# Attention in a fused two-layer kernel: the probability-times-value products issued in pairs in every second step

## The reference, cut to what matters

```python
q = jnp.einsum('bsd,hdk->bhsk', embeddings, Wq) + bq[None, :, None, :]
k = jnp.einsum('bsd,hdk->bhsk', embeddings, Wk) + bk[None, :, None, :]
v = jnp.einsum('bsd,hdk->bhsk', embeddings, Wv) + bv[None, :, None, :]
scores = jnp.einsum('bhqk,bhsk->bhqs', q, k) / jnp.sqrt(jnp.float32(dk))
scores = jnp.where(causal_mask, jnp.float32(-1000000000.0), scores)
weights = jax.nn.softmax(scores, axis=-1)
ctx = jnp.einsum('bhqs,bhsk->bhqk', weights, v)
```

## Time and profile before

| | us |
|---|---|
| median of 3 runs (1653.32 to 1657.09) | 1654.23 |
| the profiled execution, its own time | 1653.79 |
| its span in the trace | 1652.0 |
| attention stage, first to last product | 958.4 to 1438.2 |
| busy in the whole span: PE, PEld | 1332.8, 717.1 |
| busy in the whole span: DVE, ACT, POOL | 1195.5, 920.5, 932.1 |
| products (L2405), 1536 matmuls, busy | 163.7 |
| row maxima (L2103), 624 reductions, busy | 370.1 |

### The profile page before, as it was taken

How to read it: one execution, slowest core, us unless ns; L and a number is a source line. 1 busy time by engine, 2 the same in 40 slices (tenths; PEclk the granted TensorE clock), 3 DMA queues, 4 the chain that set the end, 5 groups by cost and what they waited for, 6 DMA issues and landing times. The chain is left out here.

```text
span 1652.0 us, 25211 instructions
## 1 busy us (share of the span) xinstructions
PE 1332.8 (81%) x7251; PEld 717.1 (43%) x7251; DVE 1195.5 (72%) x2207; ACT 920.5 (56%) x1736; POOL 932.1 (56%) x771
## 2 busy tenths in 40 slices
PE   5848888888788989998917999999999998812756
PEld 2313333333333359998914244444343343212643
DVE  6999999999999553233465988888888886160325
ACT  5746666666665644456566067675566666601423
POOL 2479998998999017370744021214563654874773
PEclk9879989998999978999958599999999999955867
DMA  2019100000000025786719211211221114301317
GB/s 69 0 63 345 49 0 0 0 0 0 0 0 0 1 64 153 199 242 186 206 41 262 64 32 31 61 31 31 74 64 35 44 40 106 59 10 46 105 51 255
DMA packets 123041, 124.87 MB, mean 76 GB/s; under 512 B 31182, under 2 KB 97979, under 8 KB 120304
## 3 DMA queue, kind: packets, MB, share of 16 engines
q1 hardware_dynamic: 101032, 99.70, 21.8%
q0 software_dynamic: 10240, 15.79, 3.3%
q10 hardware_dynamic: 11656, 8.00, 1.6%
HBM read 78.52 MB, written 50.91 MB: 78 GB/s over the span
## 5 line engine op out<-in xcount | busy, mean ns | idle before, releaser
L2103 DVE TENSOR_REDUCE t_negm<-t_ps 128x1 f32<-128x512 f32 (+4 forms) x624 | 370.1, 642 | 56.6 <-PE t_ps L2371 35.2
L2080 ACT ACTIVATE t_PT<-t_ps_s 128x1024 f32<-128x1024 f32 (+3 forms) x384 | 292.1, 811 | 202.5 <-PE t_ps_s L2390 201.6
L493 POOL TENSOR_TENSOR s_HC<-s_H,X 128x1024 f32<-128x1024 f32 x128 | 307.0, 2416 | 39.2 <-DVE s_H L614 31.2
L658 PE MATMUL ps_y<-s_HC,ident 128*128 128x512 f32 x512 | 262.4, 637 | 21.1 <-POOL s_HC L493 19.4
L2008 POOL TENSOR_SCALAR_AFFINE_SELECT t_PT<-t_PT 128x512 f32<-128x512 f32 x128 | 82.8, 648 | 275.9 <-ACT t_PT L2080 275.3
L2371 PE MATMUL t_ps<-heads 96*128 96x512 bf16 (+3 forms) x640 | 201.1, 341 | 9.3 <-DVE t_negm L2103 7.6
L2390 PE MATMUL t_ps_s<-heads 96*128 96x512 bf16 (+3 forms) x768 | 180.9, 328 | 4.0 <-ACT t_PT L2080 2.2
L2405 PE MATMUL t_ps_c<-t_PT,t_VG 128*32 128x512 f32 (+3 forms) x1536 | 163.7, 499 | 1.7 <-ACT t_CT L2036 1.1
L554 ACT ACTIVATE s_dA<-m_DT,s_A 128x512 f32 (+1 forms) x192 | 127.5, 712 | 60.4 <-DVE s_H L614 59.5
L658 PEld LDWEIGHTS ps_y<-s_HC,ident 128*128 128x128 f32 x512 | 94.4, 197 | 122.9 <-issue 66.8
L1992 POOL DMA_INDIRECT slots<-X,t_idx_s x128 | 127.2, 994 | 34.9 <-issue 34.3
(11 more groups left out here) (348 smaller groups left out, 2393.9 us busy)
## 6 DMA issues: line engine op xcount, KB each, us to landing
f_w<-in_W_dram SPq DMA_DIRECT2D x93, 256.0 KB, 5.5
heads<-token_expert_rows SPq DMA_DIRECT2D x8, 1024.0 KB, 9.8
token_expert_rows<-X SPq DMA_DIRECT2D x42, 192.0 KB, 2.7
heads<-q_parts SPq DMA_DIRECT2D x42, 192.0 KB
heads<-k_parts SPq DMA_DIRECT2D x14, 576.0 KB
expert_rows<-X SPq DMA_DIRECT2D x27, 192.0 KB, 2.4
f_XS<-expert_rows SPq DMA_DIRECT2D x19, 256.0 KB, 3.5
expert_rows_out<-f_YB ACTq DMA_DIRECT2D x19, 256.0 KB
```

The source lines that it names most:

```text
L493: nc.gpsimd.tensor_tensor(HC[:, g % RING], H[:, g % RING], row_wide(C_sb[:, g % RING, :], 2), ALU.mult).then_inc(s_hc, 2)
L658: nc.tensor.matmul(ps_y[c][:], ident[:], HC[:, g % RING, c, :], start=g == 0, stop=g == N - 1, skip_group_check=True).then_inc(s_y, 1)
L2080: nc.scalar.activation(PT[:, n % RP, 2 * p:2 * p + 2, 0:wd], src, ACT.Exp, scale=DK ** -0.5).then_inc(s_exp, 1)
L2103: nc.vector.tensor_reduce(out, ps_1[use % BANKS1][:, 0:h * width].rearrange("p (h k) -> p h k", h=h), AX.X, ALU.max, negate=True).then_inc ...
```

## The change

The product at x = 2 is left out in even steps. In odd steps two products are issued one behind the other: that of three blocks back and that of two blocks back. So the pairs are (10, 11) of the group before at step 1, (0, 1) at step 3, (2, 3) at step 5, (4, 5) at step 7, (6, 7) at step 9 and (8, 9) at step 11. After the last group two products are left instead of three. Waits, buffers, banks and all other engines' programs stay as they are.

```diff
@@ -2476,8 +2476,9 @@
                     for x in range(4):
                         if x < 2:
                             scores(gi, n, x)
-                        elif x == 2 and gi * NB + n >= LAG:
-                            product((gi * NB + n - LAG) // NB, (n - LAG) % NB)
+                        elif x == 2 and n % 2 and gi * NB + n >= LAG:
+                            for back in (LAG, LAG - 1):
+                                product((gi * NB + n - back) // NB, (n - back) % NB)
                         for k, (kind, i, *when) in enumerate(USES[gi]):
                             use = BEGIN[gi] + k
                             if when != [n, x]:
@@ -2494,8 +2495,8 @@
-            for n in range(LAG):
-                product(TG - 1, NB - LAG + n)
+            for n in range(LAG - 1):
+                product(TG - 1, NB - LAG + 1 + n)
```

## The result

| | before | after |
|---|---|---|
| median, us (4 runs each) | 1653.78 (1650.89 to 1657.09) | 1681.43 (1675.19 to 1686.73) |
| ratio after / before, 95% interval | | 1.0158 (1.0133 to 1.0183) |
| the profiled execution, its own time; its span | 1653.79; 1652.0 | 1683.49; 1681.7 |
| attention stage, first exponential to last product | 485.8 | 514.1 |

The change makes the kernel 27.7 us slower by the medians. The spans of the two profiled executions differ by 29.7 us, and 28.3 of these lie in the attention stage. What lies ahead of the stage is 2.5 us longer in the profiled execution after and what follows it 1.1 us shorter, and the change touches neither.

What follows compares the result with a forecast made beforehand. PE was taken to bound groups 0 to 3. Terms of 4.6 us (groups 0 to 3), 8.0 (routing groups) and 0.6 (groups 14 and 15) made 13.2, so 1653.8 became 1667; forecast 1658 to 1676, range 1640 to 1678.

Steps and rivals of the forecast that it cites:

- the discount for the routing groups: Ten groups with routing work: 0.7 of 1.15 us each, which is 0.8, and +8.0 in all.
- the term of groups 14 and 15: Groups without items: long pairs leave ACT dry, even steps catch up; +0.3 us each, between -1.4 and +1.
- the clock: TensorE's granted clock in the attention stage: read as full, with no term in the sum.
- Groups like 2: Groups 0 to 3: 2.8 us of waits, less 0.2 there already, less 1.45 saved: +1.15 us each, +4.6 together.
- Waits behind each pair: Six stretches of a group like 2: PE waits for banks or exponentials, 0.25 to 0.76 us each, 2.8 us together.
- The saving: Every pair on PE pays the 0.24 us of a product standing alone only once: 1.45 us in a group.
- The first rival: Attention stage: banks and tiles keep up, PE stays the only bound, 22.6 us come whole: 1631 us; chance 0.11.
- the fourth: Pairs on PE: second product does not follow without a hole, 94 pairs lose about 0.1 us each: 1676; chance 0.04.
- my upper bound: Groups with routing work: each loses at most 1.15 us, the loss of a group like 2.
- Masks: Products two steps behind instead of three, waiting for masks from POOL: costed at nothing, 19 us at the worst.
- The third rival: Every stretch of the groups waits 0.76 us, as the dearest does: 1694 us, or 1680 to 1694; chance 0.07.

Runs made afterwards that it cites:

- the group 9 above: The change with pairs in groups 0 to 13 alone and single products in groups 14 and 15: 1682.37 us, ratio 1.0174; group 9 took 37.23 us.
- both engines' work narrow: Row maxima over the last 128 keys, exponentials over the first 128 columns from group 1 on: 1607.51 us with single products, 1599.56 with pairs.
- the kernel with placed items and pairs in groups 0 to 3: Kernel before, with pairs and other places for the 39 items of a group, in groups 0 to 3 alone: 1652.56 us against 1654.56.

## Why the prediction was right or wrong

The direction was right and the size wrong: the forecast was 1667, the range ended at 1678, and the median is 1681.4. The stage lost 28.3 us instead of 13.2. Three steps of the sum failed: the discount for the routing groups (8.0 us too small at the full clock), the term of groups 14 and 15 (3.7 us too small), and the clock, which stood at nothing (2.4 us). The first four groups lost 1.0 us more than foretold.

**Groups like 2: right, term by term** (+5.6 measured for the four, +4.6 predicted). Waits behind each pair, from start to start less the stream:

| behind pair | (6, 7) | (4, 5) | (8, 9) | (10, 11) | (0, 1) | (2, 3) |
|---|---|---|---|---|---|---|
| predicted | 0.76 | 0.3 | 0.5 | 0.55 | 0.25 | 0.45 |
| measured | 0.76 | 0.31 | 0.63 | 0.57 | 0.28 | 0.47 |

The saving was 1.42 instead of 1.45. The only miss is (8, 9): I counted a bank for the turn of the maxima, not its wait for the joining. The first rival falls by this, and the fourth by the pair of 1.86 us: the second product follows without a hole. The Trainium skill's rule that I had set against the trace ("TensorE: Matmul & The Clock Gate", Part 3, "The mechanism") did not show here. That section of the Trainium skill names a second case too, a load to the background weight buffer; the prediction left it out, and no run here tells which buffer a load took.

**Routing groups: the discount was wrong** (+17.5 measured, +8.0 predicted). I took 0.7 of 1.15, on the ground that where VectorE sets the pace neither saving nor waits count. In groups 4, 8 and 12, at the full clock in both kernels, the saving came as in group 2 (1.41 us) and the waits were larger (3.0 us), +1.58 in all. Groups 5, 9 and 13 lose 2.0 at the full clock by the group 9 above. Groups 6 and 7 take 64.77 us after, and 62.11 where the kernel before kept the full clock (groups 10 and 11): +2.7 for two. So at the full clock the ten groups lose 3 x 1.58 + 2 x 2.66 + 3 x 1.99 = 16.0 us (taking for groups 5 and 13 what group 9 shows), all above my upper bound of 1.15 each. The bound was a group that waits less already; but the chains make VectorE late, and a late VectorE makes the waits for banks longer. In group 9 at the full clock an item at step 11 waits 1.54 us, while VectorE does four pieces of routing work ahead of the reductions:

```profile
1268.99 0.18 DVE L2207 CAST t_idxf<-t_idx 128x64 f32<-128x64 uint32 x1
1269.09 0.68 DVE L2208 TENSOR_TENSOR over<-t_LG,t_top 128x512 f32<-128x512 f32 x1
1269.70 0.66 DVE L2209 TENSOR_TENSOR t_ex<-t_top 128x32 f32<-128x32 f32 x1
1270.27 0.17 DVE L2211 COPY X<-t_idxf 128x32 f32<-128x32 f32 x1
1270.36 1.01 DVE L2103 TENSOR_REDUCE t_negm<-t_ps 128x1 f32<-128x384 f32 x2
```

```profile
1270.96 0.10 PEld L2371 LDWEIGHTS t_ps<-heads 96*128 96x128 bf16 x1 [1.54 <-DVE t_negm L2103]
```

With both engines' work narrow, pairs make groups 4, 8 and 12 0.26 us shorter, and groups 6 and 7 1.6 together. Groups 5, 9 and 13 still get 1.25 us longer: an item waits 1.18 us behind VectorE's routing chain, and the turn of the rows 0.5 us for ScalarE.

**The clock: not in the sum at all.** I read a granted clock of 1.00 in four groups and took it as given, though the trace of the kernel before had a fall to read in group 7. What a fall cost here depends on its place. The same three groups without any fall last 101.98 us (groups 9 to 11 above). Groups 5 to 7 of the change, with a fall in the middle of group 5, last 103.26: 1.3 us more. Groups 9 to 11 of the change, with two falls near the ends of groups, last 102.03, so these two cost nothing together: group 10 starts with 1.7 us less of waits for VectorE at step 0 than group 6, and group 11 with 1.2 less than group 7. In group 13, again in the middle, it is some 1.6 us (38.81 against 37.23). The fall in group 14 is some 0.9: the group takes 28.75 us, against 26.01 in the kernel with steps 3 and 4 of groups 5, 9 and 13 undone, where it has the same pairs and the full clock, and 1.8 of the 2.7 is that the turn of the maxima starts 0.7 us behind its scores there and 2.5 here. The kernel before has lost 1.4 us to its own fall in group 7 (31.25 us, against 29.84 with the same program at the full clock), which makes the difference look smaller. Together that is 1.3 + 1.6 + 0.9 - 1.4 = 2.4 us.

That the pauses bring the falls is argued, not shown. In the 13 kernels profiled, each of the 24 falls that begin inside the stage stands at or shortly behind a pause of TensorE (1.2 to 2.3 us long), and the change has nine such pauses where the kernel before has three. But about half of all such pauses have no fall: the wait of 1.3 us at the turn of the rows in group 9, as long as that in group 5, was followed by none.

**Groups 14 and 15: the term was mis-sized** (+5.2 measured, +0.6 predicted, of which the clock has 0.9). I saw that the long pairs leave ACT dry and let the even steps catch up, because ACT has 6 us of slack there. But slack over a group is not slack behind a pair. In group 15, at the full clock, ACT waits 6.3 us for scores instead of 3.7, and the scores, once TensorE is back, wait 4.6 us for ACT instead of 1.2; that group is 1.42 longer in every kernel that pairs its products and keeps the exponentials whole. The two lines of the change:

```profile
ACT t_PT L2080 <- PE t_ps_s L2390: 6.3, 6, 1.9
...
PE t_ps_s L2390 <- ACT t_PT L2080: 4.6, 12, 0.7
```

**Masks: right at nothing**, as the row above shows. The third rival, 0.76 behind every stretch, gave a time near the measured one (from 1680 up) for a reason that isn't there: only one of the six stretches waits that long.

## What to carry to other kernels

A long instruction that waits for nothing, placed between short ones that do wait, is cover: moving it together with another one saves the switch once, and uncovers what it hid. Before that is done, count what the engines beside it can hold while TensorE is away (here three banks, 1.8 us, and two tiles, 1.9 us) against the length of the new block (1.9 us), in every stage and not in the plain one alone. Slack summed over a stage does not answer that question.

## What the runs showed of the hardware

The granted clock of TensorE fell to 0.50 inside groups in which it is busy for 33.3 of 38.5 us and 22.7 of 28.8, behind pauses of 1.3 and 2.3 us, and the matmuls behind them ran at 1.2 GHz: the eight turns of the rows took 1.78 us instead of 1.09. Where it fell differed between executions of the same instructions: group 9 lasted 38.55 us with a fall near its end and 37.23 without, and groups 9 to 11 together 102.03 and 101.98. A longer one stood in group 14 of the kernel with placed items and pairs in groups 0 to 3: with the same single products as in the kernel before, the group took 27.56 us instead of 24.95 (mean clock 0.88 and 1.00).
